# Two stages of a routed feed-forward kernel: combines cut in two parts and placed on other tiles, statistics placed one or two tiles later

## The chip, the cores and the metric

The kernel runs on one core of one Trainium2 chip. The metric is the time of one execution on the device in microseconds. The kernel before takes 1050.04 us as the median of 3 runs, the lowest 1045.64 us and the highest 1051.05 us.

The core has five engines that run their own instruction streams in order and meet through semaphores: TensorE (PE, the matmuls), VectorE (DVE), ScalarE (ACT), GpSimd (POOL) and SyncE (SP, which only starts transfers).

## The reference, cut to what matters

The input x has 4096 tokens of 128 features. Four layers follow, each added to x after a layer norm of x. The change touches how the first one is added and how the second one is prepared.

```python
x = x + _L0_xattn_ref(_layernorm(x), ctx, ...)   # top 2 of 8 experts, ReLU, 128 -> 512 -> 128
x = x + _L0_ffn_ref(_layernorm(x), ...)          # top 4 of 16 experts in 2 of 4 groups, silu(x W1) * (x W3)
x = x + _L1_xattn_ref(_layernorm(x), ctx, ...)   # attention, 16 heads
x = x + _L1_ffn_ref(_layernorm(x), ...)          # quantized feed-forward

# first layer, for each token
scores_topk, idx_topk = top_k(context @ Wg + bg, 2)
weights = softmax(scores_topk)
out = sum over the two experts of weights * (relu(x @ W1 + b1) @ W2 + b2)

# second layer, for each token
s = sigmoid(x @ Wg.T); group_scores = max of s in each of 4 groups; keep 2 groups, then 4 experts
y = sum over the chosen experts of w * ((silu(x W1 + b1) * (x W3 + b3)) W2 + b2)
```

## The kernel before, in words

The tokens are held in SBUF as `X`: eight blocks of 512 tokens, each block four tiles of 128 tokens. Both routed layers are done in two halves of four blocks. A token is copied to slots sorted by expert (layer 1) or by expert group (layer 2), so that a tile of 128 slots has one expert or one group.

**The ReLU stage (layer 1)** has 78 tiles of slots, 39 in each half. In the loop over tiles `n` (`T` is the number within a half), PE multiplies tile n+2 up (lines 1915 to 1917), turns tile n+1 (L1925) and multiplies tile n down (L1937, L1939). ACT takes the ReLU (`zb`, L1571) and the high part of the turned values (`hh`, L1577), and DVE takes the low part (`hl`, L1147). Every second tile DVE adds up a pair of results (`yo`, L1155). Where `T` is a multiple of 4, a group of four new slots is turned (L1900) and split into high (ACT, L1565) and low (DVE `xTl`, L1131) parts.

**The gated stage (layer 2)** has 70 tiles, 35 in each half. In iteration `m` PE runs up(m+1), with six matmuls (L2036 to L2044), turn(m) (L2052) and down(m-1) (L2067, L2069). ACT runs silu and two scalings of tile m+1 (`sg`, L1669 and L1675), then the high part `hh` of tile m (L1682). DVE runs the gate of tile m+1 (`zb`, L1269 and L1272), then the low part `hl` of tile m (L1280). PE can turn tile m only after the gate of tile m and the low part of tile m-1. Where `T` is a multiple of 4 DVE also splits four slots (`xTl`) and picks their weights (L1136, L1139), some 1.3 us.

**The background.** Between these tiles runs the work for the next layer, block by block, placed by tables of tile numbers. `background(0, T)` runs in the second half of the ReLU stage for blocks 0 to 3, `background(1, T)` in the first half of the gated stage for blocks 4 to 7. For a block the steps are:

1. GpSimd gathers the block's result rows of layer 1 into `yg` (`gather_a`, 8 indirect transfers, L657).
2. `CMB`: DVE adds the two rows of each token to `X`, each times its gate (`combine_a`, 8 instructions on L1031, first the four for choice k = 0, then the four for k = 1).
3. `STT`: DVE takes mean and variance (`stats`, L956 to L962), which count the semaphore `var_s`.
4. GpSimd takes the reciprocal root (`power`, L611). This is in GpSimd's own order of work: power(0) and power(1) stand behind gather_a(2), power(4) behind gather_a(5), with gather_slots of the next group and gather_a(6) behind power(4).
5. `APP`: DVE computes `nbias` (`shifts`, L980), and ACT writes the normed rows to `wide` in two portions at T and T+1 (L1516).
6. `FWD`, `LOG`: PE turns the rows (L1958) and multiplies them with the router's weights (L1963).

`gather_a(b)` waits until `combine_a(b-2)` is done, since `yg` has two buffers. In the first gated half DVE also adds the second layer's bias part, `add_b2`, to a block at T = 1, 3, 5, 7 (L1105). SP clears 6 MB of SBUF (`region<-nought`, L529) once the second group of gated results is ready, on the same DMA engines that the gathers use.

## Time and profile before

| | before |
|---|---|
| median of 3 runs | 1050.04 us |
| lowest, highest | 1045.64, 1051.05 us |
| span of the profiled execution | 838.0 us |
| median less the span | 212.0 us |
| PE busy | 742.5 us, 89% of the span |
| DVE busy | 635.1 us, 76% |
| ACT busy | 502.4 us, 60% |
| POOL busy | 399.2 us, 48% |
| mean granted TensorE clock | 0.971 |

The span runs from the first to the last instruction. The profile has no time of its own for the whole execution beside the span, so the 212.0 us are what the median holds more than that span. Busy times are for the engines' own instructions. The text in square brackets behind a row of the timeline is the time that the engine sat idle ahead of it and what ended that time.

### The profile page before, as it was taken

What the parts mean: (1) busy time and instruction counts of PE and PEld (TensorE: products, weight loads), DVE (VectorE), ACT (ScalarE), POOL (GpSimd) and SP (SyncE); (2) the same over time, 40 slices, a digit from 0 to 9 for tenths busy, and PEclk for the clock granted to TensorE, in tenths of its full rate; (3) what the DMA queues carried; (4) which work ended last, traced back from release to release, by engine and by line L of the source; (5) the groups of instructions that cost most, each with busy time, mean ns of one, the idle gap of its engine ahead of it and who ended that gap; (6) DMA issues with size and microseconds to landing.
All of it is one profiled execution on the core that took longest, in us unless ns stands there. A gap on an engine that the chain in (4) does not pass through costs nothing.

```text
span 838.0 us, 17572 instructions
## 1 busy us (share of the span) xinstructions
PE 742.5 (89%) x5374; PEld 568.0 (68%) x5374; DVE 635.1 (76%) x1875; ACT 502.4 (60%) x990; POOL 399.2 (48%) x462
## 2 busy tenths in 40 slices
PE   6589999998988797987799999789999998997997
PEld 5477888887877686876688888545555555553775
DVE  5969765576588586779867786688888888884896
ACT  2745665565754665775466776355555555555796
POOL 5456776177002777510377760356775344555000
PEclk9689999999999999999999999899999999999899
DMA  9395689773113229212125220245555454441011
GB/s 315 107 315 182 220 295 255 264 225 86 39 51 97 70 67 370 56 28 66 51 69 154 85 69 14 77 114 135 146 135 142 118 172 123 119 124 27 13 39 51
DMA packets 96497, 106.57 MB, mean 127 GB/s; under 512 B 12724, under 2 KB 70468, under 8 KB 95127
## 3 DMA queue, kind: packets, MB, share of 16 engines
q1 hardware_dynamic: 76856, 78.04, 29.3%
q0 software_dynamic: 8608, 18.22, 8.5%
q10 hardware_dynamic: 10944, 9.18, 3.9%
q8 instruction: 49, 0.80, 0.4%
q14 instruction: 40, 0.33, 0.1%
HBM read 69.21 MB, written 36.18 MB: 126 GB/s over the span
## 4 chain that ended last, share of the span: by engine, by line
PE 49%; DVE 20%; POOL 11%; issue 9%; DMA 5%; ACT 4%; SPq 2%; DVEq 0%; ACTq 0%; POOLq 0%
POOL yg L657 5%; PE y_ps L2067 3%; PE y_ps L1937 3%; PE y_ps L2166 3%; PE hid_ps L2052 3%; PE hid_ps L2142 2%; PE hid_ps L2143 2%; PE tr_ps L2222 2%; PE hid_ps L2154 2%; POOL xr L648 2%; PE hid_ps L1925 2%; DVE negmax L1334 2%; PE hid_ps L2036 2%; DVE hl L1280 1%; POOL rstd L789 1%
## 5 line engine op out<-in xcount | busy, mean ns | idle before, releaser
L648 POOL DMA_INDIRECT xr<-b_tokens,idx_sb x70 | 67.3, 962 | 115.9 <-DVE idx_sb L909 94.7
L1937 PE MATMUL y_ps<-region,hh 128*128 x312 | 83.6, 345 | 11.6 <-DVE hl L1147 10.9
L1334 DVE TENSOR_REDUCE negmax<-hid_ps 128x4 f32<-128x512 f32 x128 | 85.6, 684 | 6.3 <-PE hid_ps L2143 5.9
L1147 DVE TENSOR_TENSOR hl<-hid_ps,hh 128x512 fp32r<-128x512 f32 x78 | 53.8, 690 | 46.9 <-ACT hh L1577 46.0
L657 POOL DMA_INDIRECT yg<-a_rows,idx_a x64 | 61.3, 958 | 39.5 <-issue 39.5
L679 POOL DMA_INDIRECT yg<-b_rows,idx_b x64 | 61.8, 966 | 37.9 <-issue 36.1
L2143 PE MATMUL hid_ps<-region 128*128 128x512 f32 x128 | 75.7, 594 | 0.0
L2067 PE MATMUL y_ps<-region,hh 128*128 x280 | 75.5, 347 | 0.1
L1571 ACT ACTIVATE zb<-hid_ps 128x512 f32<-128x512 f32 x78 | 46.4, 595 | 43.7 <-PE hid_ps L1917 41.9
L1937 PEld LDWEIGHTS y_ps<-region,hh 128*128 128x128 f32 x312 | 59.2, 190 | 18.3 <-issue 18.2
L1939 PE MATMUL y_ps<-region,hl 128*128 x312 | 69.7, 224 | 0.0
L1669 ACT ACTIVATE sg<-hid_ps 128x512 f32<-128x512 f32 x70 | 41.9, 598 | 46.0 <-PE hid_ps L2038 44.3
L1269 DVE TENSOR_TENSOR zb<-hid_ps,sg 128x256 f32<-128x256 f32 x70 | 29.7, 424 | 51.4 <-ACT sg L1675 49.4
L771 POOL TENSOR_SCALAR_AFFINE_SELECT sg<-sg 128x512 f32<-128x512 f32 x64 | 40.6, 634 | 58.7 <-ACT sg L1735 58.7
L1735 ACT ACTIVATE sg<-hid_ps 128x512 f32<-128x512 f32 x64 | 38.3, 598 | 43.6 <-PE hid_ps L2154 41.9
L2069 PE MATMUL y_ps<-region,hl 128*128 x280 | 63.0, 225 | 0.0
L2052 PE MATMUL hid_ps<-ident,zb 128*128 128x128 f32 x280 | 43.4, 278 | 19.6 <-DVE hl L1280 19.4
L1939 PEld LDWEIGHTS y_ps<-region,hl 128*128 128x128 f32 x312 | 60.2, 193 | 0.0
L1735 ACT ACTIVATE zb<-hid_ps 128x512 f32<-128x512 f32 x64 | 37.8, 597 | 36.3 <-PE hid_ps L2154 35.2
L2142 PE MATMUL hid_ps<-maskq,ident 128*128 128x512 bf16 x128 | 50.1, 391 | 9.9 <-DVE negmax L1334 9.2
L2052 PEld LDWEIGHTS hid_ps<-ident,zb 128*128 128x128 f32 x280 | 33.6, 142 | 33.9 <-DVE zb L1272 24.8
L771 POOL TENSOR_SCALAR_AFFINE_SELECT zb<-zb 128x512 f32<-128x512 f32 x64 | 41.1, 652 | 31.0 <-ACT zb L1735 30.2
(359 smaller groups left out, 2296.1 us busy)
## 6 DMA issues: line engine op xcount, KB each, us to landing
region<-k_strips SPq DMA_DIRECT2D x128, 64.0 KB
region<-k_strips SPq DMA_DIRECT2D x32, 256.0 KB, 3.0
region<-hl SPq DMA_DIRECT2D x128, 64.0 KB
k_strips<-k_halves SPq DMA_DIRECT2D x24, 256.0 KB
region<-nought SPq DMA_DIRECT2D x6, 1024.0 KB, 14.0
a_rows<-yo SPq DMA_DIRECT2D x20, 256.0 KB, 3.4
b_rows<-yo SPq DMA_DIRECT2D x18, 256.0 KB, 2.1
staged<-a_w_in SPq DMA_DIRECT2D x16, 256.0 KB, 6.0
```

The lines of the kernel that those rows point to most:

```text
L648: g.indirect_dma_start(xr[:, q % 3, j * RB:j * RB + w], None, src, bass.IndirectOffsetOnAxis(ap=rows.bitcast(U32), axis=0)).then_inc(x_til ...
L657: g.indirect_dma_start(yg[:, b % 2, k, j * P:(j + 1) * P], None, ys[h], bass.IndirectOffsetOnAxis(ap=idx[:, h, k, t:t + 1].bitcast(U32), a ...
L771: g.affine_select(out=prob[b], in_=prob[b], compare_op=ALU.is_gt, fill=0.0, base=1, pattern=[[0, HG], [P, P]], channel_multiplier=-(P + 1) ...
L1334: v.tensor_reduce(negmax[:, s % 2, b, :], hid_ps[b % 2][:].rearrange("p (i k) -> p i k", i=HG), AX, ALU.max, negate=True).then_inc(c_max, 1)
L1735: a.activation(prob[b], hid_ps[2 + b % 2][:], ACT.Exp, scale=float(HD) ** -0.5).then_inc(c_exp, 1)
L1937: t.matmul(y[:, c0:c0 + 2 * P], hh[:, n % 2, cs], w2a[:, bass.ds(e * (2 * FA) + c * 2 * P, 2 * P)], start=c == 0, stop=False)
L1939: t.matmul(y[:, c0:c0 + P], hl[:, n % 2, cs], w2a[:, bass.ds(e * (2 * FA) + c * 2 * P, P)], start=False, stop=False)
L2052: ins = t.transpose(hid_ps[3][:, es], zb[:, m % 2, es], ident[:])
L2067: t.matmul(y[:, c0:c0 + 2 * P], hh[:, m % 2, es], w2b[:, bass.ds(g * (2 * BT) + e * 2 * P, 2 * P)], start=e == 0, stop=False)
L2069: ins = t.matmul(y[:, c0:c0 + P], hl[:, m % 2, es], w2b[:, bass.ds(g * (2 * BT) + e * 2 * P, P)], start=False, stop=e == EG - 1)
L2142: t.matmul(hid_ps[b % 2][:], ident16[:], spread(maskq[:], [0, HG], [1, P]), start=True, stop=False)
L2143: t.matmul(hid_ps[b % 2][:], qp[s % QPS][:, b * P:(b + 1) * P], kdiag[s % KDS][:, b, :], start=False, stop=True).then_inc(c_s1, 1)
```

## The change

A combine becomes two calls, `combine_a(b, 0)` and `combine_a(b, 1)`, of four instructions each. A second set of tile numbers places the second part. `a_sum` now counts 2 for a block, and the waits on it count accordingly. Statistics of blocks 0, 1, 2, 4, 5 and 6 are placed later (7, 10, 14 become 8, 11, 15; 4, 8, 12 become 6, 10, 13), those of blocks 3 and 7 stay. For blocks 4 and 5 the shift, the normed rows, the turn and the logits come one tile later as well. Both parts of the combine stay on the same tile for blocks 3, 6 and 7.

```diff
-        CMB = ((6, 9, 13, 18), (3, 7, 11, 15))
-        STT = ((7, 10, 14, 19), (4, 8, 12, 16))
-        APP = ((11, 13, 17, 20), (7, 11, 15, 17))
...
+        CMB = (((6, 9, 13, 18), (3, 7, 11, 15)), ((7, 10, 14, 18), (5, 9, 11, 15)))
+        STT = ((8, 11, 15, 19), (6, 10, 13, 16))
+        APP = ((11, 13, 17, 20), (8, 12, 15, 17))
...
                 if b >= 2:
-                    pool.wait_ge(a_sum, b - 1)
+                    pool.wait_ge(a_sum, 2 * (b - 1))
...
-                pool.wait_ge(a_sum, NB)
+                pool.wait_ge(a_sum, 2 * NB)
...
-            def combine_a(b):
+            def combine_a(b, k):
                 h, i = divmod(b, BH)
-                eng.wait_ge(y_ld[b % 2], 16 * 2 * NT * (b // 2 + 1))
-                for k in range(2):
-                    for j in range(NT):
...
-                    if k == 0:
-                        link(ins)
+                if k == 0:
+                    eng.wait_ge(y_ld[b % 2], 16 * 2 * NT * (b // 2 + 1))
+                for j in range(NT):
...
                 ins.then_inc(a_sum, 1)
-                eng.wait_ge(a_sum, b + 1)
+                eng.wait_ge(a_sum, 2 * b + k + 1)
...
-                    if T == CMB[h][i]:
-                        combine_a(b)
+                    for k in range(2):
+                        if T == CMB[k][h][i]:
+                            combine_a(b, k)
```

Where lines moved, the changed kernel's line numbers are one or two lower (L1268 is the line that was L1269, L1279 was L1280, L1145 was L1147, L1515 was L1516).

First, VectorE in the ReLU stage's second half, tiles 9 to 11 of the kernel before. `X<-yg,gates,X` is the combine of block 1, `st` to `vepss` its statistics, `nbias` the shift of block 0, and `hl` the low part of a tile.

```order
L1031 SCALAR_TENSOR_TENSOR X<-yg,gates,X 128x128 x8
L1147 TENSOR_TENSOR hl<-hid_ps,hh 128x512
L956 BN_STATS st<-X 128x6 x4
L958 MEMSET carry 128x1
L960 BN_AGGR mvs<-st 128x2 x4
L962 TENSOR_SCALAR vepss<-mvs 128x4
L1147 TENSOR_TENSOR hl<-hid_ps,hh 128x512
L1155 TENSOR_TENSOR yo<-yo,y_ps 128x256
L980 SCALAR_TENSOR_TENSOR nbias<-mvs,rstds 128x4
```

The same place in the changed kernel:

```order
L1031 SCALAR_TENSOR_TENSOR X<-yg,gates,X 128x128 x4
L1145 TENSOR_TENSOR hl<-hid_ps,hh 128x512
L1031 SCALAR_TENSOR_TENSOR X<-yg,gates,X 128x128 x4
L1145 TENSOR_TENSOR hl<-hid_ps,hh 128x512
L1153 TENSOR_TENSOR yo<-yo,y_ps 128x256
L980 SCALAR_TENSOR_TENSOR nbias<-mvs,rstds 128x4
L956 BN_STATS st<-X 128x6 x4
L958 MEMSET carry 128x1
L960 BN_AGGR mvs<-st 128x2 x4
L962 TENSOR_SCALAR vepss<-mvs 128x4
```

A low part now stands between the combine's two parts, and the statistics of block 1 stand behind the shift of block 0 instead of ahead of it.

Second, VectorE in the first gated half, tile 4 of the kernel before and the first instruction of tile 5. `zb` is a gate, `small` and `w` the picked weights, `st` to `vepss` the statistics of block 4.

```order
L1155 TENSOR_TENSOR yo<-yo,y_ps 128x256
L1131 TENSOR_TENSOR xTl<-tr_ps,xTh 128x512
L1136 TENSOR_TENSOR small<-xr,gsel 128x16 x4
L1139 TENSOR_REDUCE w<-small 128x16
L956 BN_STATS st<-X 128x6 x4
L958 MEMSET carry 128x1
L960 BN_AGGR mvs<-st 128x2 x4
L962 TENSOR_SCALAR vepss<-mvs 128x4
L1269 TENSOR_TENSOR zb<-hid_ps,sg 128x256
```

The changed kernel, where these statistics now are, in tile 6, with the end of tile 5 ahead:

```order
L1103 TENSOR_TENSOR X<-X,cb_ps 128x512
L1031 SCALAR_TENSOR_TENSOR X<-yg,gates,X 128x128 x4
L1268 TENSOR_TENSOR zb<-hid_ps,sg 128x256
L1271 SCALAR_TENSOR_TENSOR zb<-hid_ps,w,sg 128x128 x2
L1279 TENSOR_TENSOR hl<-hid_ps,hh 128x512
L1153 TENSOR_TENSOR yo<-yo,y_ps 128x256
L956 BN_STATS st<-X 128x6 x4
L958 MEMSET carry 128x1
L960 BN_AGGR mvs<-st 128x2 x4
L962 TENSOR_SCALAR vepss<-mvs 128x4
```

The statistics of block 4 now come after two more gates, two more low parts, one `add_b2` and the second part of the combine. GpSimd's power(4) waits for them.

Third, ScalarE in the first gated half around tiles 7 and 8 of the kernel before. `wide<-X,nbias,rstds` are normed rows of block 4, and the first of them waits for `nbias` from VectorE. `sg<-hid_ps` is the silu of a tile.

```order
L1682 ACTIVATE hh<-hid_ps 128x512
L1516 ACTIVATE wide<-X,nbias,rstds 128x127 x2
L1669 ACTIVATE sg<-hid_ps 128x512
L1675 ACTIVATE sg<-sg,w 128x128 x2
L1682 ACTIVATE hh<-hid_ps 128x512
L1586 ACTIVATE yo<-y_ps 128x256
L1565 ACTIVATE xTh<-tr_ps 128x512
L1516 ACTIVATE wide<-X,nbias,rstds 128x127 x2
L1669 ACTIVATE sg<-hid_ps 128x512
```

The changed kernel, tiles 8 and 9:

```order
L1585 ACTIVATE yo<-y_ps 128x256
L1564 ACTIVATE xTh<-tr_ps 128x512
L1515 ACTIVATE wide<-X,nbias,rstds 128x127 x2
L1668 ACTIVATE sg<-hid_ps 128x512
L1674 ACTIVATE sg<-sg,w 128x128 x2
L1681 ACTIVATE hh<-hid_ps 128x512
L1515 ACTIVATE wide<-X,nbias,rstds 128x127 x2
L1668 ACTIVATE sg<-hid_ps 128x512
```

The first two rows of a block, which wait for `nbias`, now stand on the tile that also splits four slots, with a silu right behind them. The same holds for block 5 at tiles 12 and 13.

## Rows read from the trace of the kernel before

**Rows 1.** The page: busy times, and the chain that ended last

```profile
PE 742.5 (89%) x5374; PEld 568.0 (68%) x5374; DVE 635.1 (76%) x1875; ACT 502.4 (60%) x990; POOL 399.2 (48%) x462
PE 49%; DVE 20%; POOL 11%; issue 9%; DMA 5%; ACT 4%; SPq 2%; DVEq 0%; ACTq 0%; POOLq 0%
```

**Rows 2.** Waits, 160 to 200 us: who waited for whom, total, times, longest

```profile
PE y_ps L1937 <- DVE hl L1147: 4.0, 5, 1.5
```

**Rows 3.** Timeline of DVE, ReLU stage: start, duration, engine, line, operation

```profile
178.74 2.32 DVE L1031 SCALAR_TENSOR_TENSOR X<-yg,gates,X 128x128 f32<-128x128 f32 x8 [0.88 <-DMA yg<-a_rows,idx_a]
...
187.95 2.37 DVE L1031 SCALAR_TENSOR_TENSOR X<-yg,gates,X 128x128 f32<-128x128 f32 x8 [0.91 <-DMA yg<-a_rows,idx_a]
...
195.47 0.16 DVE L980 SCALAR_TENSOR_TENSOR nbias<-mvs,rstds 128x4 f32<-128x4 f32 x1 [2.10 <-POOL rstds L611]
197.55 0.69 DVE L1147 TENSOR_TENSOR hl<-hid_ps,hh 128x512 fp32r<-128x512 f32 x1 [1.91 <-ACT hh L1577]
```

**Rows 4.** Timeline of POOL, ReLU stage

```profile
164.30 0.97 POOL L657 DMA_INDIRECT yg<-a_rows,idx_a  x1 [20.45 <-issue]
...
194.40 2.04 POOL L611 TENSOR_TENSOR rstds<-vepss,mhalf 128x4 f32<-128x4 f32 x2
196.62 1.01 POOL L657 DMA_INDIRECT yg<-a_rows,idx_a  x1 [0.18 <-issue]
```

**Rows 5.** Waits, 200 to 235 us

```profile
PE y_ps L1937 <- DVE hl L1147: 0.6, 2, 0.4
```

**Rows 6.** Timeline of POOL, first gated half

```profile
306.02 1.04 POOL L611 TENSOR_TENSOR rstds<-vepss,mhalf 128x4 f32<-128x4 f32 x1
...
321.20 0.95 POOL L657 DMA_INDIRECT yg<-a_rows,idx_a  x1 [0.30 <-issue]
```

**Rows 7.** Timeline of DVE, first gated half

```profile
299.97 0.87 DVE L956 BATCH_NORM_STATS2 st<-X 128x6 f32<-128x128 f32 x4
...
301.29 0.18 DVE L962 TENSOR_SCALAR vepss<-mvs 128x4 f32<-128x4 f32 x1
...
303.63 0.42 DVE L1269 TENSOR_TENSOR zb<-hid_ps,sg 128x256 f32<-128x256 f32 x1
...
305.09 0.41 DVE L1155 TENSOR_TENSOR yo<-yo,y_ps 128x256 f32<-128x256 f32 x1
...
328.08 2.32 DVE L1031 SCALAR_TENSOR_TENSOR X<-yg,gates,X 128x128 f32<-128x128 f32 x8 [3.68 <-DMA yg<-a_rows,idx_a]
...
334.97 0.42 DVE L1269 TENSOR_TENSOR zb<-hid_ps,sg 128x256 f32<-128x256 f32 x1
```

**Rows 8.** Timeline of PE, first gated half

```profile
318.25 0.63 PE L2052 MATMUL hid_ps<-ident,zb 128*128 128x128 f32 x4 [1.20 <-DVE hl L1280]
...
332.12 1.02 PE L2052 MATMUL hid_ps<-ident,zb 128*128 128x128 f32 x4 [4.14 <-DVE hl L1280]
...
336.89 0.60 PE L2052 MATMUL hid_ps<-ident,zb 128*128 128x128 f32 x4
...
346.94 0.63 PE L2052 MATMUL hid_ps<-ident,zb 128*128 128x128 f32 x4 [0.37 <-DVE hl L1280]
...
351.49 0.63 PE L2052 MATMUL hid_ps<-ident,zb 128*128 128x128 f32 x4 [1.19 <-DVE hl L1280]
```

**Rows 9.** Timeline of ACT, first gated half

```profile
302.85 0.69 ACT L1675 ACTIVATE sg<-sg,w 128x128 f32<-128x128 f32 x2
...
327.65 0.87 ACT L1516 ACTIVATE wide<-X,nbias,rstds 128x127 f32<-128x127 f32 x2
328.41 0.59 ACT L1669 ACTIVATE sg<-hid_ps 128x512 f32<-128x512 f32 x1
```

**Rows 10.** Stretches of 4 us: busy of each engine, PE clock, DMA share, GB/s

```profile
316.00:320.00 4.00, 2.80 (x21) 2.31 (x20) 3.33 (x15) 2.40 (x6) 2.92 (x4) 1.00 0.92 338
...
332.00:336.00 4.00, 3.88 (x19) 3.83 (x20) 3.85 (x21) 0.95 (x2) 2.85 (x4) 0.57 0.88 331
```

**Rows 11.** Timeline of SP's queue, 290 to 360 us

```profile
314.27 3.31 SPq L529 DMA_DIRECT2D region<-nought  x6
```

**Rows 12.** Line 657: shortest, median and longest of its instructions

```profile
L657 POOL DMA_INDIRECT yg<-a_rows,idx_a x64: 940/950/1086, 164.3 to 337.3; - x64
```

More of the change, by code:

```diff
@@ L1022, in _ @@
             biased_a(1)
-            def combine_a(b):
+            def combine_a(b, k):
                 h, i = divmod(b, BH)
-                eng.wait_ge(y_ld[b % 2], 16 * 2 * NT * (b // 2 + 1))
-                for k in range(2):
-                    for j in range(NT):
-                        t = i * NT + j
-                        xs = X[:, b * BT + j * P:b * BT + (j + 1) * P]
-                        ins = v.scalar_tensor_tensor(xs, yg[:, b % 2, k, j * P:(j + 1) * P], gates[:, h, k, t:t + 1], xs,
-                                                     op0=ALU.mult, op1=ALU.add)
-                    if k == 0:
-                        link(ins)
+                if k == 0:
+                    eng.wait_ge(y_ld[b % 2], 16 * 2 * NT * (b // 2 + 1))
+                for j in range(NT):
+                    t = i * NT + j
+                    xs = X[:, b * BT + j * P:b * BT + (j + 1) * P]
+                    ins = v.scalar_tensor_tensor(xs, yg[:, b % 2, k, j * P:(j + 1) * P], gates[:, h, k, t:t + 1], xs,
+                                                 op0=ALU.mult, op1=ALU.add)
                 ins.then_inc(a_sum, 1)
-                eng.wait_ge(a_sum, b + 1)
+                eng.wait_ge(a_sum, 2 * b + k + 1)
             def combine_b(b):
```

4 lines of the change are left out of this document (2 added, 2 removed).

## The prediction

> **What bounds the kernel now.** I read the page's busy times and chain first, then the waits of the two stretches that the change touches, then the timelines of VectorE, GpSimd, TensorE and ScalarE there. PE is busy 89% of the span and holds 49% of the chain; GpSimd is busy 48% and still holds 11% [rows 1]. That 11% is what matters here, since much of it lies in exactly these two stretches.
>
> In the ReLU stage (160 to 200 us) PE loses 4.0 us in five waits for low parts `hl`, the longest 1.5 us [rows 2]. Two of them come from the long combines, 2.32 and 2.37 us of VectorE, with a low part queued behind [rows 3]. At first sight that is what a split would win. But the next row says more: at 195.47 VectorE stands at the shift of block 0 and has been idle for 2.10 us, waiting for GpSimd's reciprocal root [rows 3]. GpSimd started its gathers at 164.30 and goes from one to the next until power(0) and power(1) at 194.40, both together 2.04 us, followed by the gather of block 3 at 196.62, which needs only 0.18 us of its own [rows 4]. It waits for no combine and for no statistics there. So 195.47 is set by GpSimd, and whatever VectorE saves before it only lengthens its wait.
>
> In the first gated half the picture repeats. At 328.08 VectorE starts the combine of block 6 (tile 11) after 3.68 us of idle time, which a gather ended [rows 7], and PE stands 4.14 us for it, until 332.12 [rows 8]. The last of that block's gathers was issued at 321.20 [rows 6], 6.88 us earlier. That lag is long because SP started clearing 6 MB at 314.27 [rows 11]: the DMA engines are at 0.92 of their time from 316 to 320 and still at 0.88 from 332 to 336 [rows 10]. GpSimd again has no idle time in brackets ahead of power(4) at 306.02 [rows 6]: it arrives there by its own pace, block 4's statistics having ended at 301.29 + 0.18 = 301.47 [rows 7]. This slack, 306.02 - 301.47 = 4.55 us, is what the change spends.
>
> **The change part by part.** No instruction of any size is added: the combine is 64 instructions before and after, only one more count and wait at the middle of a block.
>
> *ReLU stage, tiles 6 to 10.* The splits of blocks 0 and 1 let a low part through half a combine, 1.17 us, earlier. The first part of each still waits for the gather, at 178.74 and 187.95, as now [rows 3]. All of it lies ahead of 195.47 and is worth 0. It is worth at most the 4.0 us of rows 2 if GpSimd's pace did not set 195.47. Could the second part delay GpSimd? The combine of block 0 would end near 182.9 (178.74, half a combine 1.16, a low part 0.69, a pair 0.41, a fold of the same 512 columns 0.69, half a combine 1.16). Block 2's gathers are the last 8 of the 24 from 164.30 to 194.40, a pitch of 1.25 [rows 4], and start near 184.4. That is hidden with 1.5 us to spare.
>
> *Tile 11, statistics behind the shift.* Block 1's statistics, 1.50 us (299.97 to 301.47 for the same instructions in rows 7), now start at 195.47 + 0.16 and end at 197.13. The low part behind them waits for ScalarE until 197.55 anyway [rows 3], so VectorE loses nothing, with 0.42 us of margin. Power(1) and block 3's gathers come about 1.8 us later (197.2 + 1.0 + 0.2 instead of 196.62). Block 3 is combined seven tiles further on, so this is hidden too. If its cover went, it would cost up to 1.8 us.
>
> *Tiles 13 to 15.* PE waits only 0.6 us for low parts from 200 to 235 us, in two waits [rows 5], and the block combined last there keeps its places. I take 0, bounds -0.6 and +0.4 (a margin missed). The ReLU stage together: 0.
>
> *Gated stage, block 4.* Its statistics go from tile 4 to tile 6. The gate of tile 7 waits for ScalarE's scaling, which ends at 302.85 + 0.69 = 303.54 [rows 9]; it cannot start much before its 303.63 of now, and the pair `yo` then ends at 305.01 + 0.41 = 305.42 instead of 305.50 [rows 7]. Then 1.50 us of statistics: 306.92. GpSimd is there at 306.02, so power(4), the group gathered behind it and all eight gathers of block 6 come 0.9 us later. This is the largest certain term. Bounds: 0 (if PE gets ahead enough that tile 6 comes a microsecond sooner) and 1.5 (the whole length of the statistics). The last gather of block 6 is then issued at 322.1, and with the same lag the combine starts at 328.98. The clearing starts up to 1.3 us earlier, but the lag of that gather lies inside it either way.
>
> *What is won on tiles 3 to 10*, such as PE's 1.20 us at 318.25 [rows 8], lies ahead of this wait of 3.68 us and is given back in it. The same wait hides that ScalarE's first rows of block 4 now wait for a shift behind the slot split of tile 8.
>
> *Tile 12.* Here there is no cover, since PE goes without a wait from 332.12 to 346.94 [rows 8]. Before, ScalarE had written block 5's rows (327.65) and the silu of tile 14 (328.41) during the long wait [rows 9]. Now the first rows of block 5 wait for the shift on tile 12, which stands behind combine, gate, low part, pair and slot split. From 328.08 to the gate of tile 14 at 334.97 were 6.89 us, 1.50 of them statistics that leave this tile: 5.39. So the shift starts at 328.98 + 5.4 = 334.4; with 0.16 for it, 0.87 for the rows, 0.59 for the silu, 0.69 for the scaling (durations of rows 9) the gate of tile 14 starts at 336.7 instead of 334.97. ScalarE's high part (0.59, the silu's size) and VectorE's low part (0.69) follow the scaling and the gate, and PE turns tile 14 at about 338.3 instead of 336.89: 1.4 us later, the 0.9 from before included. By then PE has also not yet done the turn of block 5, four 128x128 turns like the 0.60 us at 336.89 [rows 8], of which I count 0.4 since they overlap what follows; it now comes a tile later: 1.8. Against it, PE's clock is at 0.57 on average from 332 to 336 [rows 10], which is half speed for some 3.4 us; if 0.9 us of that now falls into the wait, 0.4 is not lost. Net 1.4. Bounds: 0 and 2.4.
>
> *Later tiles* keep their places: the waits of 0.37 and 1.19 us at 346.94 and 351.49 [rows 8] belong to block 7, whose combine and statistics have not moved.
>
> The sum is 0 + 1.4 us, on a profiled span of 838.0 us, so 839.4 us. The profile gives no time beside the span; the 212.0 us that the median holds more are not touched. 1050.04 + 1.4 = 1051.4 us.
>
> A rule speaks against part of this. VectorE's combines read two operands from SBUF, and the Trainium skill (SBUF — State Buffer, section SBUF: two separate sides) says that such an instruction and a GpSimd instruction that reads SBUF exclude each other on a shared pair of ports, each for its full length. By it, placing combines on more tiles could make more gathers wait, by up to a combine instruction each. Here the 64 gather instructions took 940 to 1086 ns with a median of 950, those under a combine included [rows 12]; by the rows this is worth nothing. By the rule alone the sum would grow by some tenths of a microsecond.
>
> **The rivals.** *The cover is complete*: power(4) is not late, the chain of waits at tile 12 is absorbed, and the time stays at 1050.0. For it speaks that my 0.9 us hang on one estimate of where tile 6 ends; against it, that 1.50 us of statistics must fit into less than 0.6 us between pair and power(4) (306.02 - 305.42).
>
> *The change wins what it aims at*: PE's waits for low parts go and no gather holds VectorE. It would be worth 4.0 + 1.20 + 0.37 + 1.19 = 6.8 us, so 1043.3. For it speak those rows; against it the idle times of 2.10 and 3.68 us, which a faster VectorE cannot shorten, and that two of the four terms belong to tiles that stay.
>
> *The slower one: ScalarE held behind the shift.* Its place is tiles 8 and 12, where rows that wait for `nbias` stand in order ahead of a silu, and PE's next tile ahead needs that silu. If PE has not the 3.68 us of cover at tile 8, it stands for the slot split, 1.3 us; and each of the two waits can bring another stretch at half clock as at 332 us, (1 - 0.57) x 4 = 1.7 us. 1.4 + 1.3 + 1.7 + 1.7 = 6.1, so 1056.1. It decides from the point where an additional wait is long enough to lower the clock: 4.14 us did [rows 8, 10], 1.20 us at 318.25 did not, the clock from 316 to 320 being 1.00 [rows 10]. The Trainium skill (TensorE: Matmul & The Clock Gate, section Part 1: The HAM clock gate) has the same order, half rate after an idle stretch and full rate after a busy one, and it gives no other price.
>
> **How the numbers follow.** My forecast has 0.5, the complete cover 0.3, the win 0.08, the slower rival 0.12. A difference under 0.5%, 5.25 us, is what a measurement of this kernel can hardly tell from none; its three runs lie 5.4 us apart. Forecast and complete cover are both inside. Within 0.5%: 0.80. Faster by more: 0.07. Slower by more: 0.13, since of the slower rival nearly all lies there and a bit of the forecast's scatter. The range is 1044.5 to 1056.5: from most of the way to the win to just beyond the slower rival. The forecast's own is 1050 to 1053.
>
> **What would show it.** Right: the shift of block 0 still starts near 195.5 after an idle time of over 3 us; GpSimd's power(4) has an idle time ahead of it ended by VectorE's `vepss`, about 0.9 us; the combine of block 6 starts near 329 and after a longer idle time than 3.68 us; ScalarE waits for `nbias` on tile 12 for several microseconds. Wrong: block 6's combine starts before 328, or PE's clock falls in more stretches than before, or VectorE's `hl` at 197.55 comes later by a microsecond, which would mean that the statistics behind the shift are not covered. The forecast as a whole is wrong if the ends of the two stages move by more than 3 us either way.

## The result and the profile after

The changed kernel takes 1041.19 us (median of 6 runs, 1039.24 to 1045.89) beside 1048.88 us for the kernel before (6 runs, 1045.64 to 1051.98). The ratio is 0.9929, 95% interval 0.9901 to 0.9958: faster by 0.7%. The prediction, 1051.4 us with a range of 1044.5 to 1056.5, was wrong.

The page of the kernel before came from an execution with a span of 838.0 us, while the timed runs take some 1049 us. The page after is of a run of 1045.89 us. So the two pages may not be subtracted from each other, and the first thing that they show is how the two lengths differ. Busy times and chain of the kernel after:

```profile
PE 803.4 (77%) x5374; PEld 612.7 (59%) x5374; DVE 638.6 (61%) x1875; ACT 501.9 (48%) x990; POOL 396.6 (38%) x462
PE 48%; another core or an unknown queue 17%; DVE 15%; issue 9%; ACT 5%; POOL 3%; DMA 1%; SPq 0%; ACTq 0%; DVEq 0%; POOLq 0%
```

Against [rows 1], DVE, ACT and POOL are busy as long as there, and PE 60.9 us longer (803.4 - 742.5), at a mean granted clock of 0.876 instead of 0.971. For PE the rest of the 206 us between the spans is idle time. 17% of the chain is put down to "another core or an unknown queue", which [rows 1] has not at all; what these waits are is shown below. POOL's share of the chain fell from 11% to 3%. The waits of POOL say why (columns: who waits for whom, us in total, times, longest):

```profile
POOL rstds L611 <- DVE vepss L962: 97.3, 12, 23.4
POOL yg L657 <- DMA a_rows<-yo: 49.8, 1, 49.8
```

In the execution of 838 us the first of these waits was about a third of that:

```profile
POOL rstds L611 <- DVE vepss L962: 35.2, 6, 13.4
```

The timeline of POOL in the ReLU stage and in the first gated half, the rows that answer to [rows 4, 6]:

```profile
257.96 0.94 POOL L657 DMA_INDIRECT yg<-a_rows,idx_a  x1 [15.35 <-DVE X L1031]
273.38 1.01 POOL L611 TENSOR_TENSOR rstds<-vepss,mhalf 128x4 f32<-128x4 f32 x1 [4.28 <-DVE vepss L962]
...
418.62 1.03 POOL L611 TENSOR_TENSOR rstds<-vepss,mhalf 128x4 f32<-128x4 f32 x1 [23.37 <-DVE vepss L962]
```

In [rows 4] GpSimd went from gather to gather without a wait and VectorE waited for it. Here it stands 15.35 us for block 0's combine, 4.28 us for block 1's statistics and 23.37 us for block 4's. The one engine on whose pace the prediction was built waits, in an execution of this length, for the engine that the change relieves. The clearing by SP, which answers to [rows 11], and the gathers of line 657, which answer to [rows 12], are much as before:

```profile
424.64 3.75 SPq L529 DMA_DIRECT2D region<-nought  x6
```

```profile
L657 POOL DMA_INDIRECT yg<-a_rows,idx_a x64: 941/947/1297, 222.6 to 456.9; - x64
```

Where the idle time lies is seen at the start of the first gated half, in the timelines of PE, DVE and ACT of the kernel after, with POOL's last gather below:

```profile
378.50 0.60 PE L2051 MATMUL hid_ps<-ident,zb 128*128 128x128 f32 x4
...
383.27 0.40 PE L2043 MATMUL hid_ps<-region,xTh 128*128 x1
397.44 1.08 PE L2051 MATMUL hid_ps<-ident,zb 128*128 128x128 f32 x4 [13.78 <-issue]
```

```profile
387.69 0.42 DVE L1268 TENSOR_TENSOR zb<-hid_ps,sg 128x256 f32<-128x256 f32 x1 [8.89 <-remote]
388.03 0.60 DVE L1271 SCALAR_TENSOR_TENSOR zb<-hid_ps,w,sg 128x128 f32<-128x128 f32 x2
396.60 0.69 DVE L1279 TENSOR_TENSOR hl<-hid_ps,hh 128x512 fp32r<-128x512 f32 x1 [7.97 <-issue]
```

```profile
395.97 0.60 ACT L1681 ACTIVATE hh<-hid_ps 128x512 fp32r<-128x512 f32 x1 [13.47 <-remote]
```

```profile
394.30 0.95 POOL L657 DMA_INDIRECT yg<-a_rows,idx_a  x1 [0.30 <-issue]
```

From 388.6 to 396.0 TensorE, VectorE and ScalarE all stand. Two of them wait for the third: TensorE's next turn needs VectorE's low part `hl`, and that needs ScalarE's high part `hh`, so that the three go on one behind the other from 395.97 to 397.44. ScalarE waits for TensorE's turn, which began at 378.50, took 0.60 us and had ended at 379.10, and its own work before ended at 382.5. The trace's semaphore records tell what ended this wait: the semaphore on which only TensorE's turns count has its event at 395.95, 16.9 us after that end, though TensorE had started its next product at 382.01. The profile calls such a wait "remote", since it looks for the counting instruction only in the last 1.5 us. In the eight long traces (this one and those of groups 1 and 2 below) each "remote" wait of over 1 us, 327 in all, is of ScalarE or VectorE for a count that only TensorE's instructions make, with the event 1.5 to 24.1 us behind the recorded end of the last such instruction; in one trace they add up to 184 to 235 us. In the twelve short traces there is none. Since TensorE's ends are modelled, the records do not decide in each case whether the matmul or its count was late. The late `hh` starts just after the last gather of a long row of them ends at 395.25.

I counted the common idle time of the three engines through the routed stages, in stretches of over 0.3 us. In the eight traces with spans of 1022 to 1053 us (this one and those of groups 1 and 2 below, 45 to 690 us) it is 89 to 103 us, over half of it (54 to 64%) under a gather instruction, where these cover 34% of that time. Rows of gathers that stand under 0.4 us apart cover 44% of it, and 168 of the 186 stretches of over 1.5 us begin in such a row. In the execution of 838 us (45 to 500 us) there is no common idle stretch of over 0.3 us.

The whole difference in length lies there. From the first low part of the ReLU stage to the end of the last one of the gated stage pass 481.1 us in the execution of 838 us and 680.6 us in this one, while the parts ahead of it (49.1 and 50.3 us) and behind it (307.8 and 313.1 us) differ little. In the same part half of the semaphore records is missing (4,019 against 7,832).

### The profile page after: what moved, and what is told of

Same layout as the page of the kernel before. It is cut to its first block, busy times and chain, and to the rows that moved or that the text cites. A ratio compares the mean times of both kernels' runs of the same rounds, so it can differ in the third digit from the quotient of the medians.

```text
span 1044.0 us, 17576 instructions
## 1 busy us (share of the span) xinstructions
PE 803.4 (77%) x5374; PEld 612.7 (59%) x5374; DVE 638.6 (61%) x1875; ACT 501.9 (48%) x990; POOL 396.6 (38%) x462
## 4 chain that ended last, share of the span: by engine, by line
PE 48%; another core or an unknown queue 17%; DVE 15%; issue 9%; ACT 5%; POOL 3%; DMA 1%; SPq 0%; ACTq 0%; DVEq 0%; POOLq 0%
PE y_ps L1936 4%; PE y_ps L2066 3%; PE y_ps L2165 3%; PE hid_ps L2051 3%; PE hid_ps L1924 2%; PE hid_ps L2153 2%; PE hid_ps L2141 2%; PE hid_ps L2142 2%; PE hid_ps L1914 2%; PE tr_ps L2221 2%; PE hid_ps L2035 2%; PE hid_ps L1916 1%; PE y_ps L2068 1%; PE y_ps L1938 1%
## 5 line engine op out<-in xcount | busy, mean ns | idle before, releaser
L648 POOL DMA_INDIRECT xr<-b_tokens,idx_sb x70 | 67.2, 959 | 155.5 <-DVE idx_sb L909 100.8
L1936 PE MATMUL y_ps<-region,hh 128*128 x312 | 91.8, 371 | 35.5 <-issue 19.5
L1145 DVE TENSOR_TENSOR hl<-hid_ps,hh 128x512 fp32r<-128x512 f32 x78 | 53.9, 690 | 104.7 <-ACT hh L1576 57.7
L2051 PE MATMUL hid_ps<-ident,zb 128*128 128x128 f32 x280 | 49.3, 305 | 64.2 <-issue 39.8
L1936 PEld LDWEIGHTS y_ps<-region,hh 128*128 128x128 f32 x312 | 64.8, 208 | 44.0 <-issue 43.8
L1268 DVE TENSOR_TENSOR zb<-hid_ps,sg 128x256 f32<-128x256 f32 x70 | 29.7, 424 | 97.7 <-ACT sg L1674 52.2
L2051 PEld LDWEIGHTS hid_ps<-ident,zb 128*128 128x128 f32 x280 | 37.7, 157 | 80.9 <-issue 57.3
L2066 PE MATMUL y_ps<-region,hh 128*128 x280 | 85.0, 379 | 0.1
L1570 ACT ACTIVATE zb<-hid_ps 128x512 f32<-128x512 f32 x78 | 46.5, 596 | 74.3 <-PE hid_ps L1916 38.3
L1668 ACT ACTIVATE sg<-hid_ps 128x512 f32<-128x512 f32 x70 | 41.8, 597 | 79.0 <-PE hid_ps L2037 43.4
L1681 ACT ACTIVATE hh<-hid_ps 128x512 fp32r<-128x512 f32 x70 | 40.9, 584 | 73.9 <-remote 59.1
L1279 DVE TENSOR_TENSOR hl<-hid_ps,hh 128x512 fp32r<-128x512 f32 x70 | 47.9, 684 | 41.5 <-issue 26.9
L1938 PE MATMUL y_ps<-region,hl 128*128 x312 | 73.2, 235 | 0.0
L1924 PE MATMUL hid_ps<-ident,zb 128*128 128x128 f32 x312 | 51.8, 293 | 23.8 <-ACT zb L1570 14.3
L2068 PE MATMUL y_ps<-region,hl 128*128 x280 | 66.9, 239 | 0.0
L1938 PEld LDWEIGHTS y_ps<-region,hl 128*128 128x128 f32 x312 | 66.0, 212 | 0.0
L1924 PEld LDWEIGHTS hid_ps<-ident,zb 128*128 128x128 f32 x312 | 41.7, 152 | 39.0 <-ACT zb L1570 17.1
```

The costliest lines, as they stand in the source:

```text
L648: g.indirect_dma_start(xr[:, q % 3, j * RB:j * RB + w], None, src, bass.IndirectOffsetOnAxis(ap=rows.bitcast(U32), axis=0)).then_inc(x_til ...
L1145: v.tensor_tensor(hl[:, n % 2, :], hid_ps[2 + n % 2][:], hh[:, n % 2, :].bitcast(F32), ALU.subtract).then_inc(a_hl, 1)
L1924: ins = t.transpose(hid_ps[2 + n % 2][:, cs], zb[:, n % 2, cs], ident[:])
L1936: t.matmul(y[:, c0:c0 + 2 * P], hh[:, n % 2, cs], w2a[:, bass.ds(e * (2 * FA) + c * 2 * P, 2 * P)], start=c == 0, stop=False)
L1938: t.matmul(y[:, c0:c0 + P], hl[:, n % 2, cs], w2a[:, bass.ds(e * (2 * FA) + c * 2 * P, P)], start=False, stop=False)
L2051: ins = t.transpose(hid_ps[3][:, es], zb[:, m % 2, es], ident[:])
```

## Experiments

The runs fell into five groups, each with its own runs of the kernel before on the same chip. That kernel took 1049.31 us in group 1, 1036.48 in group 2, and 843.95, 843.57 and 841.96 in groups 3 to 5. Both lengths are thus found in timed runs, and each ratio below is against the runs of its own group. By their numbers the chips of the five groups are 2, 6, 4, 2 and 6, so chip 2 and chip 6 each appear once long and once short; the two long groups are the first two in time. I call 1036 to 1049 us long and 842 to 844 us short.

### Group 1, long: the change, and each half of it alone

*c_before* is the kernel before, unchanged, *c_after* the changed one. *e_relu* has the changed tables in the ReLU stage and the old ones in the gated stage, *e_gated* the reverse. Both are shown against the changed kernel:

```diff
# e_relu
-        CMB = (((6, 9, 13, 18), (3, 7, 11, 15)), ((7, 10, 14, 18), (5, 9, 11, 15)))
-        STT = ((8, 11, 15, 19), (6, 10, 13, 16))
+        CMB = (((6, 9, 13, 18), (3, 7, 11, 15)), ((7, 10, 14, 18), (3, 7, 11, 15)))
+        STT = ((8, 11, 15, 19), (4, 8, 12, 16))
# e_gated
+        CMB = (((6, 9, 13, 18), (3, 7, 11, 15)), ((6, 9, 13, 18), (5, 9, 11, 15)))
+        STT = ((7, 10, 14, 19), (6, 10, 13, 16))
```

(and APP, FWD and LOG of the gated stage accordingly). Expected:

> The kernel before, unchanged. The page shown of it has a span of 838.0 us against a median of 1048.88 us, while the changed kernel's profiled execution spans 1044.0 us and was timed at 1045.89 us. Theory G (the page shown was of an unusual execution, in which engines never stood for long): this run spans 1040 to 1052 us, its mean clock is 0.87 to 0.89, ScalarE and PE have many idle times of 4 to 14 us, GpSimd stands before power(0) and power(4) for VectorE's vepss, and block 6's combine has no 3.68 us wait for a gather. Rival H (the change itself brings those long idle times and something else pays for them): this run spans about 840 us again. Ratio to the kernel before: 1.000 within 0.003.

> The changed kernel again, as the scale for the others on this chip. Theory G: 0.990 to 0.996 of the kernel before, since VectorE's saved time is not given back at GpSimd where GpSimd waits. Rival P (long idle times fall at other places and the 0.7% is chance of where they fall): the ratio lies anywhere from 0.990 to 1.003, and the trace differs from that of the kernel before in stages that the change does not touch.

> Only the ReLU half is changed (second parts of the combines on tiles 7, 10, 14, statistics on 8, 11, 15); in the first gated half both parts stand together and the tables are those of before. Theory G: about half of the gain, 0.995 to 0.998. My prediction's theory (GpSimd sets the shift of block 0, nothing is won here): 1.000.

> Only the first gated half is changed (second parts on tiles 5 and 9, statistics on 6, 10, 13, shift, turn and logits of blocks 4 and 5 one tile later); the ReLU half has both parts together and the tables of before. Theory G: the rest of the gain, 0.995 to 0.998, additive with the ReLU half. My prediction's theory: 1.001 to 1.002, since power(4) is late and ScalarE waits behind the shift on tile 12.

Measured: c_before 0.9991 (0.9956 to 1.0025), c_after 0.9917 (0.9886 to 0.9948), e_relu 0.9955 (0.9934 to 0.9976), e_gated 0.9957 (0.9924 to 0.9991). The gain is there again, each half carries about half of it, and the halves add up. The theory of the prediction, by which both halves are covered by GpSimd, falls for this length. In the kernel before too GpSimd waits for VectorE at power(1) and at power(4), as the timeline of POOL in c_before shows:

```profile
276.55 1.01 POOL L611 TENSOR_TENSOR rstds<-vepss,mhalf 128x4 f32<-128x4 f32 x1 [6.07 <-DVE vepss L962]
...
421.68 1.04 POOL L611 TENSOR_TENSOR rstds<-vepss,mhalf 128x4 f32<-128x4 f32 x1 [19.71 <-DVE vepss L962]
```

How long the touched tiles take is read from VectorE's timeline, from the low part `hl` of tile 0 of the ReLU stage's second half to that of tile 18. The kernel before:

```profile
221.22 0.69 DVE L1147 TENSOR_TENSOR hl<-hid_ps,hh 128x512 fp32r<-128x512 f32 x1 [1.27 <-ACT hh L1577]
...
300.73 0.69 DVE L1147 TENSOR_TENSOR hl<-hid_ps,hh 128x512 fp32r<-128x512 f32 x1 [1.39 <-ACT hh L1577]
```

and the changed kernel in the same group:

```profile
221.85 0.69 DVE L1145 TENSOR_TENSOR hl<-hid_ps,hh 128x512 fp32r<-128x512 f32 x1 [1.27 <-ACT hh L1576]
...
297.80 0.69 DVE L1145 TENSOR_TENSOR hl<-hid_ps,hh 128x512 fp32r<-128x512 f32 x1 [1.52 <-ACT hh L1576]
```

79.5 us become 76.0. Read in the same way, and from tile 1 to tile 18 of the first gated half:

| kernel | group | ReLU tiles 0 to 18, us | gated tiles 1 to 18, us |
|---|---|---|---|
| c_before | 1, long | 79.5 | 87.1 |
| c_after | 1 | 76.0 | 82.8 |
| e_relu | 1 | 76.0 | 87.3 |
| e_gated | 1 | 78.5 | 84.3 |
| after | measured pair, long | 76.0 | 89.1 |
| e_split | 2, long | 73.1 | 88.1 |
| e_stats | 2 | 79.8 | 84.9 |
| f_more | 2 | 74.6 | 85.2 |
| before | the page, short | 51.5 | 68.6 |
| c_after2 | 3, short | 53.1 | 70.2 |
| c_after3 | 4, short | 53.4 | 70.3 |
| e_relu2 | 5, short | 51.6 | 68.7 |
| e_gated2 | 5 | 50.4 | 70.3 |
| g_mix | 3 | 50.2 | 70.5 |
| d_before, d_before2 | 3, 4 | 45.8, 45.8 | 64.6, 64.6 |
| d_after, d_after2 | 3, 4 | 44.9, 44.9 | 67.8, 67.2 |
| p_all, p_all2 | 4, 5 | 45.8, 45.8 | 65.6, 65.7 |

What did not shrink is the wait that answers to [rows 2, 5], TensorE's for low parts, in most of these same tiles of c_before (232 to 301 us) and of c_after (231 to 298 us):

```profile
PE y_ps L1937 <- DVE hl L1147: 3.9, 3, 2.5
```

```profile
PE y_ps L1936 <- DVE hl L1145: 6.0, 5, 3.2
```

In the long executions the ReLU stage is 2.5 to 3.5 us shorter with the changed tables than with the old ones; three traces with them agree on 76.0. In the gated stage it is 2.8 to 4.5 us within group 1, but single traces scatter there more than that: the `after` trace has 89.1. The trace of c_before is of its slowest execution, 1054.62 us beside a median of 1048.72, so that the differences from it may be too large; against e_gated, with the old tables in the ReLU stage, it is 2.5 us.

### Group 2, long: the split alone, the statistics alone, more splits

*e_split* has only the split, *e_stats* only the later steps, *f_more* splits blocks 3, 6 and 7 too:

```diff
# e_split
+        CMB = (((6, 9, 13, 18), (3, 7, 11, 15)), ((7, 10, 14, 18), (4, 8, 11, 15)))
         STT, APP, FWD, LOG as in the kernel before
# e_stats
+        CMB = (((6, 9, 13, 18), (3, 7, 11, 15)), ((6, 9, 13, 18), (3, 7, 11, 15)))
         STT, APP, FWD, LOG as in the changed kernel
# f_more
+        CMB = (((6, 9, 13, 18), (3, 7, 11, 15)), ((7, 10, 14, 19), (5, 9, 12, 16)))
```

> Only the split of the combines; statistics, shifts, turns and logits on the tiles of the kernel before (second parts on tiles 7, 10, 14 and 4, 8). Split theory: what wins is that a low part or a gate passes between the two halves of a combine, 1.15 us earlier; then this keeps most of the 0.8% of the whole change, ratio 0.993 to 0.996. Statistics theory: what wins is that 1.5 us of statistics leave the tile right behind a combine (in the gated stage a tile that also splits four slots); then this is worth 0.2% or less, ratio 0.998 to 1.001, and may lose, because combine part, statistics and, in the gated stage, the slot split now stand together on tiles 4 and 8.

> Only the statistics (and the shift, rows, turn and logits of blocks 4 and 5) moved as in the change; each combine stays whole on its first tile. Statistics theory: most of the gain, ratio 0.992 to 0.995. Split theory: little of it, 0.998 to 1.000. If both parts carry about the same, both runs come to 0.995 to 0.997.

> The whole change and the same split for two more blocks: second part of block 3 on tile 19 instead of 18, of block 6 on tile 12 instead of 11 of the gated stage, and of block 7 on 16 instead of 15 (statistics where they are). Split theory: each gives about 0.5 to 1 us more than the whole change, so 1038 to 1040 us where the whole change takes 1040.7, ratio 0.989 to 0.991. Statistics theory: no further gain, or a loss of 1 to 2 us, since on tiles 12 and 16 of the gated stage the second part stands with the slot split, and on 19 and 16 right ahead of the statistics: 1041 to 1043 us, 0.992 to 0.994.

Measured: e_split 0.9989 (0.9961 to 1.0016), e_stats 0.9985 (0.9956 to 1.0015), f_more 0.9944 (0.9917 to 0.9972). Neither theory got its numbers: neither part alone can be told from no change. The traces hint at a place for each, the split in the ReLU stage (73.1 against 79.8 us) and the later statistics in the gated stage (84.9 against 88.1), but this is not shown: there is one trace of each, that of e_split is of its fastest execution (1024.18 us, median 1034.30) and that of e_stats of its slowest (1043.25, median 1035.15), and group 2 has no trace of the kernel before. Whether the two parts need each other stays open, since the whole change was not run in a long group beside them. f_more did not come out better than the whole change had in group 1.

### Group 3, short: the whole change again, a mixture, and plain transfers

*c_after2* is the changed kernel. *g_mix* is f_more with the old statistics in the ReLU stage (STT 7, 10, 14, 19). *d_before* and *d_after* take the gather by index out of line 657, so that other rows are added to `X` and the second layer routes other values:

```diff
-  g.indirect_dma_start(yg[:, b % 2, k, j * P:(j + 1) * P], None, ys[h],
-                       bass.IndirectOffsetOnAxis(ap=idx[:, h, k, t:t + 1].bitcast(U32), axis=0))
+  g.dma_start(yg[:, b % 2, k, j * P:(j + 1) * P], ys[h][(2 * t + k) * P:(2 * t + k + 1) * P, :])
```

> The changed kernel once more, as the measure beside the others of this call. Its two parts alone came to 0.9989 and 0.9985, where the whole came to 0.9917 in another call. If the parts add up, this is 0.997 (with 0.9946 to 1.000 for it by their intervals); if they need each other, or if the whole change simply does better, it is 0.991 to 0.994 again.

> The whole change, with blocks 3, 6 and 7 split too (tiles 19, 12, 16), but in the ReLU stage the statistics on the tiles of the kernel before (7, 10, 14). If in the ReLU stage the split alone does the work and the later statistics do not, this is at least as good as the whole change with the further splits (0.9944): 0.991 to 0.994. If the later statistics are needed there too, it is 0.996 to 0.998.

> The kernel before, with the 64 indirect gathers of the first layer's result rows replaced by plain transfers of the same size on the same queue (so the rows added are the wrong ones, and the second layer routes other values). In the traces of ordinary length all three of TensorE, VectorE and ScalarE stand idle at once in some 20 to 27 stretches of over 1.5 us, 82 to 92 us in all, and most begin while GpSimd issues gathers back to back. If the gathers' issue causes them, those in tiles 0 to 18 of the ReLU stage's second half and 0 to 15 of the gated stage go (some 15 to 30 us of the 80 to 90), and the kernel takes 1010 to 1035 us where before takes 1036 to 1049, ratio 0.97 to 0.99. Rival: the stretches come from the data moved or from something else; then they stay, and the ratio is 0.995 to 1.005.

> The changed kernel with the same plain transfers instead of gathers. If the change gains by what VectorE's long pieces cost the tiles, it gains here as well, 3 to 8 us against the run with plain transfers of the kernel before. If its gain is tied to the long idle stretches that come with the gathers (combines that no longer fall into them), the two runs with plain transfers are equal within 2 us.

Measured: c_after2 1.0049 (1.0023 to 1.0076), g_mix 1.0051 (1.0024 to 1.0077), d_before 0.9911 (0.9886 to 0.9935), d_after 0.9923 (0.9895 to 0.9952). None of the expectations had thought of this: the group is short, and here the change makes the kernel slower by 3.5 us (847.42 against 843.95). That is the length of which the prediction had its page, so its steps can be held against this trace one by one. The ReLU stage of c_after2, DVE, POOL and PE:

```profile
200.41 0.16 DVE L980 SCALAR_TENSOR_TENSOR nbias<-mvs,rstds 128x4 f32<-128x4 f32 x1 [3.69 <-POOL rstds L611]
```

```profile
202.05 1.01 POOL L611 TENSOR_TENSOR rstds<-vepss,mhalf 128x4 f32<-128x4 f32 x1 [1.68 <-DVE vepss L962]
```

```profile
202.01 0.66 PE L1924 MATMUL hid_ps<-ident,zb 128*128 128x128 f32 x4 [2.92 <-ACT zb L1570]
```

Tile 0's low part starts at 165.52 in this trace and at 160.94 in the one before. So the shift of block 0 comes 34.89 us into the stage, where [rows 3] have 195.47 - 160.94 = 34.53, and the wait ahead of it has grown from 2.10 to 3.69 us: what the split won was given back there, as forecast. But the longer wait had a price of its own. Stretches of 5 us of this trace (columns as in [rows 10]):

```profile
199.50:204.50 5.00, 1.83 (x9) 1.60 (x10) 2.78 (x13) 3.90 (x9) 2.90 (x3) 0.82 0.24 69
204.50:209.50 5.00, 5.00 (x23) 4.60 (x23) 2.61 (x8) 3.03 (x7) 3.79 (x4) 0.50 0.20 52
```

and of the kernel before at the same place:

```profile
195.00:200.00 5.00, 2.92 (x18) 2.22 (x17) 1.69 (x4) 4.12 (x10) 4.21 (x5) 0.91 0.40 95
200.00:205.00 5.00, 5.00 (x31) 4.51 (x30) 4.52 (x16) 3.20 (x8) 3.78 (x5) 0.75 0.19 52
```

PE stood 2.92 us instead of 1.42 and then ran the 5 us from 204.5 at 0.50, which is 1.2 GHz, with 23 matmuls in place of 31. The Trainium skill (TensorE: Matmul & The Clock Gate, section Part 1: The HAM clock gate) has half rate after an idle stretch; the trace agrees, and it adds the price. The whole stretch at half clock is 6.8 us long here:

```profile
202.69:209.52 6.83, 6.19 (x27) 5.80 (x28) 3.71 (x10) 4.84 (x11) 5.18 (x6) 0.50 0.14 38
```

Each of the six short traces with the gathers has one such stretch in this stage. In g_mix, e_gated2, before and e_relu2 it is 3.4 us long, ahead of it PE had stood 1.61, 1.92, 1.42 and 2.46 us, and the stages take 50.2, 50.4, 51.5 and 51.6 us. In c_after2 and c_after3 it is 6.8 us long, after 2.92 and 3.45 us, and the stages take 53.1 and 53.4 us. In e_gated2 it comes early, before VectorE's wait for `rstds`:

```profile
192.20:195.60 3.40, 3.40 (x15) 3.00 (x15) 1.95 (x10) 0.38 (x1) 2.84 (x3) 0.50 0.22 58
```

Another 3.4 us at half clock are 1.7 us of work, about the step from 51.5 and 51.6 us to 53.1 and 53.4 us. VectorE's wait alone does not set the order: it is 2.18 us in g_mix and 1.00 in e_gated2. Nor are the stages of one program equal: before and e_gated2 have the same tables here (51.5 and 50.4 us), and so have e_relu2, c_after2 and c_after3 (51.6, 53.1 and 53.4). g_mix has the split with the old statistics and takes 50.2 us, so in this stage the loss seems to come with the later statistics; this is one trace.

The gated stage of the same trace, POOL, DVE, ACT and PE, answering to [rows 6 to 9]:

```profile
313.38 1.03 POOL L611 TENSOR_TENSOR rstds<-vepss,mhalf 128x4 f32<-128x4 f32 x1 [1.23 <-DVE vepss L962]
```

```profile
334.83 2.38 DVE L1031 SCALAR_TENSOR_TENSOR X<-yg,gates,X 128x128 f32<-128x128 f32 x8 [4.90 <-DMA yg<-a_rows,idx_a]
```

```profile
340.55 0.88 ACT L1515 ACTIVATE wide<-X,nbias,rstds 128x127 f32<-128x127 f32 x2 [6.95 <-DVE nbias L980]
```

```profile
338.93 0.82 PE L2051 MATMUL hid_ps<-ident,zb 128*128 128x128 f32 x4 [4.57 <-DVE hl L1279]
```

Power(4) waits for the later statistics, block 6's combine starts after 4.90 us of idle time instead of 3.68, and ScalarE stands 6.95 us for `nbias` on tile 12. Counted from tile 1's low part (292.25 here, 285.81 before) the combine itself starts only 0.3 us later, 42.58 us in instead of 42.27; in c_after3 and e_gated2 it is 0.8 and 0.9 us. Tiles 1 to 18 take 70.2 us instead of 68.6. The clock has a part in this too. Behind the stand for this combine, which before had 3.4 us at half clock in [rows 10], it now stays at half for 6.8 us, here and in c_after3, e_gated2 and g_mix. Stretches of 4 us of c_after2 and of before, each beginning some 3 to 4 us after PE went on:

```profile
342.00:346.00 4.00, 3.96 (x13) 3.28 (x13) 3.26 (x16) 3.20 (x9) 3.08 (x5) 0.50 0.20 54
```

```profile
336.00:340.00 4.00, 4.00 (x29) 3.67 (x28) 2.38 (x6) 2.64 (x7) 3.41 (x4) 1.00 0.23 64
```

Again 3.4 us more at half clock are 1.7 us of work, as much as these stages grew.

The plain transfers show that the gathers did set the pace in the short kind. In d_before the rows of POOL and DVE are:

```profile
193.10 1.00 POOL L611 TENSOR_TENSOR rstds<-vepss,mhalf 128x4 f32<-128x4 f32 x1 [4.66 <-DVE vepss L961]
```

```profile
193.86 0.15 DVE L979 SCALAR_TENSOR_TENSOR nbias<-mvs,rstds 128x4 f32<-128x4 f32 x1
```

```profile
L657 POOL DMA_DIRECT2D yg<-a_rows x64 | 34.6, 571 | 29.4 <-issue 22.3 <-DVE X L1030 7.1
```

Each of the 64 takes 571 ns on average, where the gathers took 958 (median 950, [rows 12]). POOL now waits for VectorE's statistics, VectorE's shift of block 0 has no wait, and the stages are 5.7 and 4.0 us shorter than in the short trace before (45.8 and 64.6 against 51.5 and 68.6).

### Group 4, short: once more, and without any gather by index in the two stages

*p_all* also turns line 648's gathers of slots into plain transfers (rows `(4 * q + j) % TH * P` onward of the token table). *d_before2*, *d_after2* and *c_after3* repeat. For p_all the slots hold other tokens.

> The kernel before, with plain transfers on the same queue in place of the indirect gathers of the slots (109) and of the first layer's result rows (64), so slots hold other tokens and the rows added are the wrong ones. On a chip of the longer kind (before at 1036 to 1049 us): if the gathers' issue causes the common idle stretches, nearly all of the 82 to 92 us go, and the kernel takes under 900 us. If they have another cause, the stretches stay and it takes 1020 us or more. On a chip where before takes 844 us: 825 to 835 us by either.

> The kernel before, with plain transfers only for the first layer's 64 result rows gathers. On the 844 us chip this gave 0.9911. On a longer chip: by the theory that gathers cause the idle stretches 0.97 to 0.99, the stretches in tiles 0 to 18 of the ReLU stage's second half and 0 to 15 of the gated stage gone; by the rival 0.995 to 1.005.

> The changed kernel with the same plain transfers. On the 844 us chip the two with plain transfers stood at 836.85 and 837.54 us. On a longer chip: a gain of 4 us or more against the other one with plain transfers if VectorE's long pieces alone make it; within 2 us if it is tied to the gathers.

> The changed kernel as it is. If the sign of the change goes with the chip: 0.990 to 0.995 where before takes 1036 to 1050 us, 1.002 to 1.008 where it takes some 844 us. If it does not, the ratio lies between, 0.996 to 1.001.

Measured: p_all 0.9849 (0.9798 to 0.9900), d_before2 0.9888 (0.9839 to 0.9937), d_after2 0.9887 (0.9838 to 0.9936), c_after3 1.0038 (1.0007 to 1.0070). The change is slower here too. With plain transfers the difference has no clear sign: 837.54 against 836.85 us in group 3, 834.78 against 836.07 in group 4. This fits that in the short kind the loss hangs on GpSimd's gathers, but does not prove it, since the intervals of these four runs are 4 to 8 us wide. The two stages go apart: with GpSimd ahead, the changed ReLU stage is 0.9 us shorter in both groups, the gated one 2.6 to 3.2 us longer, more than with the gathers; the medians of the whole do not resolve this.

The question for which p_all was made, whether the gathers' issue causes the common idle time of the long kind, was not answered: the group was short.

### Group 5, short: each half alone, and p_all again

Edits as e_relu, e_gated and p_all.

> Only the ReLU stage's half changed. Where before takes 844 us: the profiles of the two whole kernels have tiles 0 to 18 of that stage 1.6 us longer after the change (51.5 and 53.1 us), so +1.6 us, ratio 1.002 (1.000 to 1.004); by the reading of the prediction, nothing, 1.000. Where it takes 1036 us or more: 0.995 to 0.998 as before.

> Only the first gated half changed. Where before takes 844 us: the prediction has +1.4 us for this half, the two profiles have tiles 1 to 18 of it 68.6 and 70.2 us, +1.6 us; so 1.002 (1.000 to 1.004). If the loss sat in one half alone, one of these two runs would come to 1.004 and the other to 1.000. Where it takes 1036 us or more: 0.993 to 0.998.

> Plain transfers on the same queue in place of the gathers by index of slots and of the first layer's rows, in the kernel before. Where before takes 844 us this gave 0.985. Where it takes 1036 us or more: if the gathers' issue causes the common idle stretches, most of 82 to 92 us go and it takes under 960 us, ratio under 0.92; if they have another cause, 0.98 or more.

Measured: e_relu2 1.0040 (1.0015 to 1.0064), e_gated2 1.0050 (1.0027 to 1.0074), p_all2 0.9876 (0.9854 to 0.9897). Each half alone costs about what the whole cost in groups 3 and 4, so unlike the gain of the long kind the losses do not seem to add up. The profiled execution of e_relu2 shows no loss in its stage (51.6 us), and its run of 840.63 us is the fastest of its 12, which reach to 849.84 apart from one of 1695 us: the clock's answer to the wait differs from execution to execution. e_gated2 has the 1.7 us in its stage (70.3 against 68.6), as every short trace with the changed gated tables and the gathers has, 70.2 to 70.5; each of these four has 6.8 us at half clock there, where before and e_relu2 have 3.4.

## Why the prediction was wrong

**The sum's last step failed.** "The 212.0 us that the median holds more are not touched" took the time beside the span for something outside the kernel's stages. It was time of the routed stages themselves (680.6 and 690.0 us in after and c_before where the page has 481.1), in idle stretches and at a lower clock, and with it went the premise of the whole sum, that GpSimd sets the pace of both stretches. The gap was in the table of the profile before, and an execution 20% shorter than every timed run should have been read as another regime and not as the same one with a constant added.

**ReLU stage, taken as 0.** For the long kind wrong, because "it waits for no combine and for no statistics there" [rows 4] does not hold there: GpSimd waits 15.35 us and 4.28 us for VectorE in the kernel after, 15.63 and 6.07 us in c_before. The cover is absent, and the stage is 2.5 to 3.5 us shorter. For the short kind the mechanism held: shift of block 0 at the same place, wait over 3 us, and power(1) waited 1.68 us for its statistics, where the working had the gathers behind it 1.8 us later. What was missing is the clock after the lengthened wait, up to 1.9 us (53.4 - 51.5). The prediction had 4.14 us as a wait that lowers the clock and 1.20 us as one that does not; in its own trace 1.42 us at 197.08 was already followed by 3.4 us at half clock.

**Gated stage, +1.4 us.** For the short kind the steps up to tile 12 held. Power(4) waited 1.23 us (0.9 forecast), the combine of block 6 had 4.90 us ahead of it instead of 3.68 and came 0.3 to 0.9 us later (0.9 forecast), and ScalarE stood several microseconds on tile 12 as said. The stage grew by 1.6 to 1.9 us, but that this is near 1.4 is in part luck: the sum took 0.4 us off because part of the half-clock time would fall into the wait, while the stretch at half clock became twice as long, 6.8 us instead of 3.4, at a price of up to 1.7 us. For the long kind wrong by sign: power(4) waits 23.37 us there (19.71 in c_before), so the 4.55 us of slack that the change was to spend never existed. How VectorE's relief gets through is less clear than that there is no cover, since the long idle stretches fall on different tiles in each kernel.

**Whole kernel.** In short executions +0.4 to +0.5% measured, +0.1% forecast: the sign right, the size too small by 2 to 3 us, of which the clock after the longer stands in the two stages is one part; how much of it the timed executions have is not shown by single traces. In long executions -0.7 to -0.8%. Of the rivals, "the change wins what it aims at" (1043.3 us, chance 0.08) comes nearest to the measured 1041.19. It had the sign, and its objection, the idle times of [rows 3, 7], belongs to the other length; but that its mechanism was at work is not shown, since TensorE's waits for low parts, which it counts on, grew from 3.9 to 6.0 us in c_after. The rule of the Trainium skill (SBUF — State Buffer, section SBUF: two separate sides) on shared ports, which was weighed, decides nothing here: the median gather took 947 ns after the change, and in the trace before 947 ns beside a combine and 952 ns away from one.

**Open** stays what makes an execution long. The common idle time is shown, and the late counts of TensorE that end the waits of ScalarE and VectorE in it; the tie to the gathers is one of coincidence (54 to 64% of it under instructions that cover 34%, 168 of 186 long stretches beginning in a row of gathers), and the test of it ran in short groups only. A rival is the recording itself: where the idle time lies, half of the semaphore records is missing, and no run without it is on record here. The chip alone does not decide the length, since chips 2 and 6, if these numbers name the same chips throughout, each show both. Open is also by what path VectorE's relief wins time in the long kind, and whether the split and the later statistics each win by themselves.

## What to carry to other kernels

Before any row is priced, compare the span of the profiled execution with the timed runs. If they differ by more than their scatter, find where the missing time lies, or give the forecast a range that holds the case in which the pinning engine of the profile is not the pin. A cover is a statement on one regime: ask of each engine that "never waits" how many microseconds it is ahead, and what happens if its neighbours are 20% slower. And time won ahead of a wait is not simply given back: the longer wait can cost TensorE's clock afterwards.

## What the runs showed of the hardware

- The same kernel takes 842 to 844 us in three groups of runs and 1036 to 1049 us in two others, each steady within 2%, apart from single outliers. A change that gains 0.8% in the one costs 0.4 to 0.5% in the other.
- In the long kind TensorE, VectorE and ScalarE stand idle together for 89 to 103 us between 45 and 690 us, in the six short traces with the gathers 0 to 2.8 us. In the eight long traces ScalarE and VectorE waited 327 times over 1 us for a count of TensorE whose event is recorded 1.5 to 24.1 us behind the recorded end of the instruction that makes it, in no short trace once; they make up most of the 13 to 17% of the chain that the profile puts down to "another core or an unknown queue". A third of the semaphore records is missing in the long trace after (10,924 against 15,721 in the short one before), and half of them in the two routed stages (4,019 against 7,832).
- In the ReLU stage of the short kind TensorE ran 6.8 us at 0.50 of its clock after stands of 2.92 and 3.45 us, and 3.4 us at 0.50 after stands of 1.42 to 2.46 us.
- A plain 64 KB transfer on GpSimd's queue takes 571 ns of its time on average, an indirect one 958.
